# Attention values as the fixed operand in column strips, with outputs that come out turned and scaled

## The chip, the cores and the metric

One Trainium2 chip, one core. The metric is the device time of one launch in microseconds, as the median of several runs; a profile of one execution stands beside it.

## The reference

A transformer block over 4096 tokens of 256 channels, in float32. Its rows are normalised; then attention and a mixture of experts both read the normalised rows, and both are added to the input:

```python
xn = _layernorm(x, axis=-1)
x = x + attention(xn, ...) + experts(xn, ...)
```

The attention is local, with 8 heads of 32 channels. Tokens form blocks of 12, and a block's queries see their own block and the one before it (24 keys):

```python
q, k, v = xn @ Wq.T, xn @ Wk.T, xn @ Wv.T          # 8 heads of 32; q and k scaled
logits = einsum('bnchd,bnkhd->bhnck', q, k_ctx) + rel_shift(einsum('bnchd,phd->bhncp', q, rel_k))
attn = softmax(tanh(logits / 50) * 50, axis=-1)
out = einsum('bhnck,bnkhd->bnchd', attn, v_ctx) @ Wpost.T
```

The experts: each token goes to the best 2 of 8 experts (256 to 704 to 256 channels, silu gate), weighted by its routing probabilities.

## The kernel before

The program writes one instruction stream for each engine by hand; semaphores (`s_...`) order them.

*Attention part.* The tokens are cut into 38 groups (`NG`) of 9 blocks: 108 queries (`GQ`) and 120 keys (`GK`), with the blocks in an order in which even and odd ones lie apart (`ORDER`). A loop over `s` from 0 to 42 is a software pipeline, and each engine runs it in its own order: stage `s` transposes the rows of group `s+1`, makes queries, keys, value rows and position biases of group `s`, scores of group `s-3`, values of group `s-4`, and the projection and output of group `s-5`. Router logits of 4 tiles are made in each of the stages 4 to 11 (`S_L`). VectorE makes the routing in steps from stage 12 on (`S_R`); from stage 26 on (`S_OH`) its steps are eight batches of one-hot tables, which TensorE multiplies in stages 27 to 34 (`tables`). GpSimd splits one piece of expert weights in each of the stages from 8 on.

TensorE's order in a stage: `tables`, `scores(s-3)`, a logits tile, `values(s-4)`, `rows_v(s)`, `project(s-5)`, `turn_out(s-4)`, `turn_biases(s-2)`, `turn(s+1)`, `queries(s)`, `keys(s)`, `biases(s)`. Scores of one head take 32 rows of TensorE's array (`r = slice(DH * i, DH * (i + 1))`), so heads `i` = 0 to 3 lie in four row strips.

*The values.* ScalarE leaves `ex`, the exponentials, with 120 keys on the partitions and 108 queries per head in the columns. GpSimd multiplies five heads (`HM`) by the mask of block pairs, VectorE the other three, the late ones. `v1` holds 32 value columns a head and a column of ones. In `values` each head's `ex` is the fixed operand and `v1` moves 33 columns, so that PSUM bank 6 gets queries on the partitions, and in column 33 each head's denominator. VectorE takes the reciprocal of the 8 denominators and multiplies (`o_sb`, `s_o`). In `turn_out` TensorE transposes the result back, and in the same step brings the queries from the block order to the token order (`perm_out`). VectorE copies it as two parts, `oT_hi` rounded and `oT_lo` the rest, and `project` multiplies them with the two parts of the weights in three reduced-precision passes for each half of the channels. `res` adds the input rows.

```python
for h in (*range(HM, H), *range(HM)):
    if h == 0:
        pe.wait_ge(s_mk, g + 1)
    head = HC * (h % KD) + h // KD
    ins = mm(psum[0:GQ, 6, head * HV:(head + 1) * HV], ex[0:GK, g % 2, h, :], v1[0:GK, g % 5, head, :],
             True, True)
```

VectorE's order in a stage: the routing step, the reciprocal and product of group `s-4`, the late heads' mask of group `s-3`, the residual sum of group `s-5`, the two parts of `oT`, the copy of turned biases, the rest of the turned rows (`rest_v`), the copy of the keys (`kT`), which the next stage's scores wait for, and the copy of the position biases.

*Expert part.* After the loop TensorE runs the experts block by block, 128 slots at a time.

Of the kernel before, what the change touches and what calls it, by code (L numbers as in the profile page):

```python
# [6 lines left out]
ALU = mybir.AluOpType  # L7
# [6 lines left out]
P = 128  # L14
# [24 lines left out]
HV = DH + 1  # L39
# [45 lines left out]
C_OUT = C_IN + GK  # L85
C_FIRST = C_OUT + GK

# [3 lines left out]
def constants():  # L91
# [16 lines left out]
    c[np.arange(GK), C_OUT + np.roll(row, -PAST)] = 1.0  # L108
# [9 lines left out]
def program(nc, x, pos_t, wq, wk, wv, wpost, wrel, dim_scale, norm_w, router_t, w_raw, alpha, const_d,  # L118
            xn_d, bd_d, w_split, out):
    with ExitStack() as ctx:  # L120
# [19 lines left out]
        vp_w = sb("vp_w", [P, 2, 2, KD, D], F32R)  # L140
        WV, WP = range(2)
# [20 lines left out]
        turns = sb("turns", [P, P + 2 * GK], F32R)  # L162
# [3 lines left out]
        perm_out = turns[0:GK, P + GK:P + 2 * GK]  # L166
# [6 lines left out]
        turns_raw = sb("turns_raw", [P, P + (2 + len(NEAR)) * GK], at=raw_at + 2 * KD * D * 4)  # L173
        near_in = turns_raw[:, P + 2 * GK:P + (2 + len(NEAR)) * GK].rearrange("p (i n) -> p i n", n=GK)
        vp_raw = sb("vp_raw", [P, 2, KD, D], at=raw_at)
# [9 lines left out]
        def tile8(i):  # L185
# [5 lines left out]
                     shb=2 * H * CTX, rep=2 * H * DH, relT=2 * KD * GQ, v1=5 * H * HV, ex=2 * H * GQ, xw=NXW * D, o=D, res=2 * D)  # L191
# [10 lines left out]
        o_m = at_m["o"].rearrange("p (h n) -> p h n", h=H)  # L202
# [5 lines left out]
        v1 = at["v1"].rearrange("p (b h n) -> p b h n", b=5, h=H)  # L208
# [31 lines left out]
        rden = sb("rden", [P, H])  # L240
# [22 lines left out]
        s_oth = sem("s_oth")  # L263
# [55 lines left out]
        s_o = sem("s_o")  # L319
        s_ot = sem("s_ot")  # L320
# [150 lines left out]
        def _(sp):  # L471
# [6 lines left out]
            sp.dma_start(vp_raw[:, WV, :, :], wv.rearrange("(k p) e -> p k e", p=P)).then_inc(s_wv, 16)  # L478
# [5 lines left out]
            sp.wait_ge(s_ini, 6)  # L484
# [6 lines left out]
            sp.dma_start(vp_raw[:, WP, :, :], wpost.rearrange("(k p) e -> p k e", p=P)).then_inc(s_wp, 16)  # L491
# [81 lines left out]
        def _(pool):  # L573
# [45 lines left out]
            rest_vp(WV)  # L619
            pool.dma_start(x_all[:, PARTS[2][0]:PARTS[2][1], :], tile_rows(x, 2)).then_inc(s_x[2], 16)  # L620
            for s in range(NG + 3):
# [27 lines left out]
                if s == 3:  # L649
                    rest_vp(WP)  # L650
# [24 lines left out]
        def _(act):  # L675
# [25 lines left out]
            def load_raw(n):  # L701
                if n < NSPL:
                    e, cols = piece(n)
                    if n == 0:
                        act.wait_ge(s_vpl, 2)
                        act.wait_ge(s_turns, 1)
                        act.wait_ge(s_t, NWIN)
# [35 lines left out]
            round_vp(WV, s_wv)  # L743
# [40 lines left out]
            for s in range(NG + NSTEP):  # L784
# [53 lines left out]
                if s == 2:  # L838
                    round_vp(WP, s_wp)
# [37 lines left out]
        def _(dve):  # L877
# [56 lines left out]
            dve.tensor_copy(turns[:, :], turns_raw[:, 0:P + 2 * GK]).then_inc(s_turns, 1)  # L934
# [205 lines left out]
            for s in range(NG + NSTEP):  # L1140
# [476 lines left out]
```

## Time and profile before

| what | us |
|---|---|
| runs | 823.52, 826.76, 829.49 |
| median | 826.76 |
| profiled execution, device time | 825.49 |
| its span, first to last instruction | 823.7 |
| TensorE busy | 778.6 |
| VectorE busy | 458.5 |
| ScalarE busy | 344.2 |
| GpSimd busy | 408.7 |

The span is cut by time: the attention loop ends near 350 us, the experts fill the rest. Busy time of TensorE counts matmuls that overlap once; the profile shows a full-precision matmul as two records, and a reduced-precision one as one.

### The profile page before, as it was taken

The numbers are of one execution on the slowest core, as the hardware profiler recorded it, in microseconds if no ns is written. First come the engines' busy times: TensorE is split into PE (matmuls) and PEld (weight loads), VectorE is DVE, ScalarE is ACT, GpSimd is POOL, SyncE is SP. The second block draws the span as 40 slices with busy tenths as digits, with TensorE's granted clock in tenths as the row PEclk, the third lists the DMA queues.
The fourth block names the chain that finished last, engine by engine and source line by source line (L and its number), as shares of the span: only waits on it lengthen the run. The fifth ranks groups of instructions, "written<-read, shape, count | busy, mean of one in ns | idle before, by whom it ended". The sixth has DMA issues, their size and how long they took to land.

```text
span 823.7 us, 20450 instructions
## 1 busy us (share of the span) xinstructions
PE 778.6 (95%) x6909; PEld 750.2 (91%) x6909; DVE 458.5 (56%) x1057; ACT 344.2 (42%) x620; POOL 408.7 (50%) x307
## 2 busy tenths in 40 slices
PE   6599999999899999899999999999999999999993
PEld 6599999999799998899999999999999999999993
DVE  5464358888788855454444444444444444444441
ACT  4456666666545466333333333333333333333330
POOL 2777867777846667513333333333333333333322
PEclk9799999999999999799999999999999999999997
DMA  8645788899954463112264363363363462222211
GB/s 254 186 129 163 242 267 281 300 300 310 307 197 137 127 137 89 36 31 40 40 175 120 83 177 69 69 182 80 71 174 87 119 175 39 35 39 41 37 26 24
DMA packets 65798, 111.07 MB, mean 135 GB/s; under 512 B 15640, under 2 KB 47812, under 8 KB 65700
## 3 DMA queue, kind: packets, MB, share of 16 engines
q0 software_dynamic: 19536, 44.22, 22.4%
q1 hardware_dynamic: 34644, 45.03, 18.6%
q10 hardware_dynamic: 11520, 20.47, 7.5%
q8 instruction: 67, 1.10, 0.6%
q14 instruction: 31, 0.25, 0.1%
HBM read 66.97 MB, written 42.75 MB: 133 GB/s over the span
## 4 chain that ended last, share of the span: by engine, by line
PE 85%; DMA 3%; DVE 3%; issue 2%; POOL 2%; ACT 1%; ACTq 1%; SPq 1%; POOLq 0%; DVEq 0%
PE psum L1251 77%; PE psum L1359 4%; PE psum L1322 1%; POOL xn_all L611 1%; DMA arena<-in_x 1%; DMA out<-spare,sca_i 1%; DVE arena L1196 1%; PE psum L1435 1%; ACTq L752 1%; DMA q_scale<-in_dim_scale 1%; PE psum L1295 1%; PE psum L1444 1%; PE psum L1270 1%; DVE xT L1111 1%; ACT xT L755 0%
## 5 line engine op out<-in xcount | busy, mean ns | idle before, releaser
L1251 PE MATMUL psum<-w_ring,xT 128*128 x1608 | 278.4, 329 | 4.3 <-DVE xT L1111 1.5
L1251 PEld LDWEIGHTS psum<-w_ring,xT 128*128 128x128 f32 x1608 | 258.0, 189 | 17.4 <-issue 15.1
L657 POOL DMA_INDIRECT out<-spare,sca_i x67 | 106.3, 1586 | 273.7 <-DVE spare L1235 248.9
L1100 DVE SCALAR_TENSOR_TENSOR spare<-psum,xg,spare 128x704 f32<-128x704 f32 x67 | 63.7, 951 | 161.4 <-PE psum L1251 161.2
L1251 PE MATMUL psum<-w_ring,hT 128*128 x1139 | 151.6, 286 | 2.1 <-DVE spare L1235 1.4
L1251 PEld LDWEIGHTS psum<-w_ring,hT 128*128 128x128 f32 x1139 | 140.2, 190 | 2.4 <-issue 2.4
L857 ACT ACTIVATE spare<-psum,xg 128x704 f32<-128x704 f32 x67 | 56.8, 847 | 159.8 <-PE psum L1251 159.8
L755 ACT ACTIVATE xT<-psum,nwp 128x128 fp32r<-128x128 f32 x134 | 41.9, 364 | 159.0 <-PE psum L1322 142.6
L635 POOL TENSOR_TENSOR arena<-arena,const 120x540 f32<-120x540 f32 x38 | 59.9, 1576 | 71.7 <-ACT arena L801 71.6
L1251 PE MATMUL psum<-arena 32*120 32x108 f32 (+1 forms) x1216 | 87.7, 265 | 0.0
L594 POOL DMA_INDIRECT xg<-xn_d,gat_i x67 | 70.4, 1051 | 32.3 <-issue 19.1
L1251 PEld LDWEIGHTS psum<-arena 32*120 32x120 f32 (+1 forms) x1216 | 82.7, 181 | 2.8 <-issue 0.2
L585 POOL TENSOR_TENSOR w_ring<-raw,w_ring 128x1088 fp32r<-128x1088 f32 x32 | 84.7, 2646 | 0.0
L1251 PE MATMUL psum<-arena,att_w 128*128 128x120 f32 (+1 forms) x608 | 82.4, 288 | 0.0
L1251 PEld LDWEIGHTS psum<-arena,att_w 128*128 128x128 f32 x608 | 75.2, 200 | 0.0
L1111 DVE SCALAR_TENSOR_TENSOR xT<-psum,nwp,xT 128x128 fp32r<-128x128 f32 x134 | 40.9, 347 | 57.8 <-ACT xT L755 57.8
L1223 DVE TENSOR_TENSOR hT<-psum,hT 128x768 fp32r<-128x768 f32 x67 | 64.2, 958 | 7.3 <-ACT hT L865 1.5
L797 ACT ACTIVATE psum<-psum 120x864 f32<-120x864 f32 x38 | 33.3, 876 | 55.5 <-PE psum L1251 55.0
L865 ACT ACTIVATE hT<-psum 128x768 fp32r<-128x768 f32 x67 | 54.4, 811 | 4.9 <-PE psum L1359 4.9
L1359 PEld LDWEIGHTS psum<-turns,hb_m 128*128 128x128 f32 x402 | 41.4, 140 | 1.7 <-issue 0.3
L1359 PE MATMUL psum<-turns,hb_m 128*128 128x128 f32 x402 | 42.0, 241 | 0.1
L577 POOL TENSOR_TENSOR arena<-arena 120x256 f32<-120x256 f32 x38 | 31.6, 833 | 17.6 <-DMA arena<-in_x 17.5
(171 smaller groups left out, 1000.1 us busy)
## 6 DMA issues: line engine op xcount, KB each, us to landing
w_split<-w_ring POOLq DMA_DIRECT2D x20, 1088.0 KB, 6.7
w_ring<-w_split SPq DMA_DIRECT2D x40, 544.0 KB, 3.8
raw<-in_w_raw ACTq DMA_DIRECT2D x32, 544.0 KB, 5.9
arena<-xn_d SPq DMA_DIRECT2D x34, 120.0 KB
arena<-in_x SPq DMA_DIRECT2D x37, 108.0 KB
out<-arena SPq DMA_DIRECT2D x37, 108.0 KB
bd_d<-arena SPq DMA_DIRECT2D x38, 84.4 KB
xn_d<-xn_all POOLq DMA_DIRECT2D x3, 1024.0 KB, 7.5
```

The costliest lines, as they stand in the source:

```text
L585: pool.tensor_tensor(lo, raw[:, n % NST, :], hi.bitcast(F32), ALU.subtract).then_inc(s_spl, 1)
L594: pool.indirect_dma_start(out=xg[:, b % NXG, :], out_offset=None, in_=xn_d, in_offset=bass.IndirectOffsetOnAxis(ap=gat_i[:, b:b + 1], axis=0),
L635: pool.tensor_tensor(ex[0:GK, g % 2, 0:HM, :], ex[0:GK, g % 2, 0:HM, :], mask.rearrange("p (a n) -> p a n", a=1).to_broadcast([GK, HM, GQ] ...
L657: pool.indirect_dma_start(out=out, out_offset=bass.IndirectOffsetOnAxis(ap=sca_i[:, b:b + 1], axis=0), in_=y[:, b % 2, :], in_offset=None, ...
L755: ins = act.activation(xT[:, b % 2, HI, k, :], psum[:, x_bank(b), k * P:(k + 1) * P], ACT.Copy, scale=nwp[:, k:k + 1])
L857: act.activation(sg[:, b % 2, :].rearrange("p (a n) -> p a n", a=2), psum[:, 0:2, 0:HALF], ACT.Silu, scale=xg[:, b % NXG, D:D + 1]).then_i ...
L865: act.activation(hT[:, b % 2, HI, :, :].rearrange("p (a k) n -> p a (k n)", a=2), psum[:, 4:6, 0:3 * P], ACT.Copy).then_inc(s_hta, 1)
L1100: dve.scalar_tensor_tensor(out=hb[:, b % 2, 0:HID].rearrange("p (a n) -> p a n", a=2), in0=psum[:, 2:4, 0:HALF], scalar=scale, in1=sg[:, b ...
L1111: ins = dve.scalar_tensor_tensor(out=xT[:, b % 2, LO, k, :], in0=psum[:, x_bank(b), k * P:(k + 1) * P], scalar=nwp[:, k:k + 1], in1=xT[:, ...
L1223: dve.tensor_tensor(hT[:, b % 2, LO, :, :].rearrange("p (a k) n -> p a (k n)", a=2), psum[:, 4:6, 0:3 * P], hT[:, b % 2, HI, :, :].bitcast ...
L1251: return pe.matmul(out_ap, lhs, rhs, start=first, stop=last)
L1359: ins = pe.transpose(moved(psum[:, 4 + c // 3, (c % 3) * P:(c % 3 + 1) * P]), hb_m[:, b % 2, c * P:(c + 1) * P], ident_m)
```

## The change

The two operands of the values' products change places. Each head's 32 value columns are the fixed operand, and its 108 columns of `ex` move; the result lands on 32 partitions of bank 6, channels on the partitions, so the four heads of one half of the channels lie in four column strips of the array. A second product for each head, with 32 columns of ones as the fixed operand, puts the head's denominators beside it, one copy on each of the 32 partitions. So 8 products of a group become 16, and their order is: the three late heads' values, their denominators, then the other five by halves. VectorE takes the reciprocal of all 216 columns of denominators and multiplies in two steps (odd and even blocks), which write the queries in token order. The output transposes (`turn_out`, `perm_out`), `o_sb`, and the two parts of `oT` go; `oT` is double-buffered, in plain float32. `project` becomes one full-precision product for each half of the channels, with the projection weights as loaded; ScalarE's and GpSimd's steps that split those weights in stages 2 and 3 go. The fills of `v1`'s ones and of `o_sb` become one of `oT`.

```diff
-        vp_w = sb("vp_w", [P, 2, 2, KD, D], F32R)
-        WV, WP = range(2)
+        wv_w = sb("wv_w", [P, 2, KD, D], F32R)
+        wp_w = sb("wp_w", [P, KD, D])
...
-        v1 = at["v1"].rearrange("p (b h n) -> p b h n", b=5, h=H)
+        v = at["v"].rearrange("p (b h n) -> p b h n", b=5, h=H)
...
-        o_sb = at["o"].rearrange("p (h n) -> p h n", h=H)
+        rden = at["rden"][:, 0:KD * GQ]
         res = at["res"].rearrange("p (b d) -> p b d", b=2)
         xv = sb("xv", [P, 2, KD, GK], F32R)
-        oT_hi = sb("oT_hi", [P, KD, GK], F32R)
-        oT_lo = sb("oT_lo", [P, KD, GK], F32R)
+
+        oT = sb("oT", [P, 2, KD, GK])
...
-            pool.memset(v1[:, :, :, DH:HV], 1.0).then_inc(s_ini, 1)
-            pool.memset(o_sb[:, :, :], 0.0).then_inc(s_ini, 1)
+            pool.memset(oT[:, :, :, :], 0.0).then_inc(s_ini, 1)
...
-                if s == 3:
-                    rest_vp(WP)
...
-                if s == 2:
-                    round_vp(WP, s_wp)
...
-                    pv = psum[0:GQ, 6, 0:H * HV].rearrange("p (h n) -> p h n", h=H)
-                    dve.reciprocal(rden[0:GQ, :], pv[:, :, DH:HV].rearrange("p h n -> p (h n)")).then_inc(s_rc, 1)
+                    if g == 0:
+                        dve.wait_ge(s_ini, 5)
+                    if g >= 2:
+                        dve.wait_ge(s_po, g - 1)
+                    dve.reciprocal(rden, psum[:, 6, KD * GQ:2 * KD * GQ]).then_inc(s_rc, 1)
                     dve.wait_ge(s_rc, g + 1)
-                    if g:
-                        dve.wait_ge(s_ot, g)
-                    dve.tensor_tensor(o_sb[0:GQ, :, :], pv[:, :, 0:DH],
-                                      rden[0:GQ, :].rearrange("p (h n) -> p h n", n=1).to_broadcast([GQ, H, DH]),
-                                      ALU.mult).then_inc(s_o, 1)
+
+                    place = oT[:, g % 2, :, :].rearrange("p k (m a c) -> p k m a c", a=2, c=CHUNK)
+                    for first, n, m, a in ((0, NODD, 1, 0), (NODD, NEVEN, 0, 1)):
+                        cols = slice(first * CHUNK, (first + n) * CHUNK)
+                        num, den = (t.rearrange("p (k n) -> p k n", k=KD)[:, :, cols].rearrange("p k (m c) -> p k m c", c=CHUNK)
+                                    for t in (psum[:, 6, 0:KD * GQ], rden))
+                        ins = dve.tensor_tensor(place[:, :, m:m + n, a, :], num, den, ALU.mult)
+                    ins.then_inc(s_ote, 1)
...
-                    dve.wait_ge(s_ot, g + 1)
-                    if g:
-                        dve.wait_ge(s_po, g)
-                    o_ps = psum[:, 6, 0:KD * GK].rearrange("p (k n) -> p k n", k=KD)
-                    dve.tensor_copy(oT_hi[:, :, :], o_ps).then_inc(s_oth, 1)
-                    dve.wait_ge(s_oth, g + 1)
-                    dve.tensor_tensor(oT_lo[:, :, :], o_ps, oT_hi[:, :, :].bitcast(F32), ALU.subtract).then_inc(s_ote, 1)
...
-                for h in (*range(HM, H), *range(HM)):
-                    if h == 0:
-                        pe.wait_ge(s_mk, g + 1)
-                    head = HC * (h % KD) + h // KD
-                    ins = mm(psum[0:GQ, 6, head * HV:(head + 1) * HV], ex[0:GK, g % 2, h, :], v1[0:GK, g % 5, head, :],
-                             True, True)
+
+                def products(heads, of):
+                    for h in heads:
+                        i, k = h // KD, h % KD
+                        at = (KD * of + k) * GQ
+                        lhs = ones[0:GK, 0:DH] if of else v[0:GK, g % 5, HC * k + i, :]
+                        ins = mm(psum[DH * i:DH * (i + 1), 6, at:at + GQ], lhs, ex[0:GK, g % 2, h, :], True, True)
+                    return ins
+
+                late = range(HM, H)
+                products(late, 0)
+                products(late, 1)
+                pe.wait_ge(s_mk, g + 1)
+                for first in range(KD):
+                    products(range(first, HM, KD), 0)
+                    ins = products(range(first, HM, KD), 1)
...
-                    pe.wait_ge(s_vpl, 2)
+                    pe.wait_ge(s_wp, 16)
                 if g:
                     pe.wait_ge(s_r2, g)
                 for k in range(KD):
-                    for po, pw in PASSES:
-                        ins = mm(psum[0:GK, 7, 0:D], (oT_hi, oT_lo)[po][:, k, :], vp_w[:, pw, WP, k, :],
-                                 k == 0 and (po, pw) == PASSES[0], k == KD - 1 and (po, pw) == PASSES[-1])
+                    ins = mm(psum[0:GK, 7, 0:D], oT[:, g % 2, k, :], wp_w[:, k, :], k == 0, k == KD - 1)
...
-            def turn_out(g):
-
-                pe.wait_ge(s_o, g + 1)
-                for k in range(KD):
-                    ins = pe.matmul(moved(psum[:, 6, k * GK:(k + 1) * GK]),
-                                    o_m[0:GK, HC * k:HC * (k + 1), :].rearrange("p h n -> p (h n)"), perm_out,
-                                    start=True, stop=True, is_transpose=True)
-                ins.then_inc(s_ot, 1)
...
-                    turn_out(s - 4)
```

## Rows read from the trace of the kernel before

**Rows 1.** The profile's page: the chain that ended last, shares of the span by engine.
```profile
PE 85%; DMA 3%; DVE 3%; issue 2%; POOL 2%; ACT 1%; ACTq 1%; SPq 1%; POOLq 0%; DVEq 0%
```

**Rows 2.** Stretches: length, busy us (instructions) by engine, granted clock, DMA share, GB/s.
```profile
43.20:117.60 74.40, 73.67 (x868) 71.61 (x869) 35.57 (x106) 47.10 (x95) 57.57 (x48) 1.00 0.62 196
117.60:218.90 101.30, 98.44 (x1217) 94.68 (x1216) 81.75 (x212) 67.67 (x115) 76.36 (x54) 1.00 0.90 299
218.90:232.20 13.30, 8.89 (x89) 8.61 (x90) 11.50 (x15) 4.70 (x9) 7.61 (x7) 0.87 0.80 277
232.20:302.70 70.50, 70.31 (x816) 68.18 (x814) 57.08 (x116) 37.67 (x64) 43.28 (x24) 1.00 0.50 139
```

**Rows 3.** Timeline of stage 24, TensorE: start us, us, line, tiles, shape, [idle before].
```profile
204.65 0.68 PE L1251 MATMUL psum<-arena,const 32*120 32x108 f32 x16 [0.22 <-DVE arena L1196]
...
207.22 0.96 PE L1251 MATMUL psum<-vp_w,xv 128*120 128x256 f32 x6
208.02 0.40 PE L1251 MATMUL psum<-vp_w,oT_hi 128*120 128x256 f32 x2
...
208.73 0.28 PE L1444 MATMUL psum<-turns,arena_m 120*128 120x120 f32 x2
208.85 0.33 PE L1435 MATMUL psum<-turns,arena_m 108*128 108x108 f32 x2
...
209.19 2.02 PE L1251 MATMUL psum<-arena,att_w 128*128 128x108 f32 x16
...
211.80 0.63 PE L1251 MATMUL psum<-arena,const 32*120 32x108 f32 x13 [0.22 <-DVE arena L1196]
```

**Rows 4.** Timeline of stage 26 and the start of stage 27, TensorE and VectorE.
```profile
226.81 0.20 DVE L1153 RECIPROCAL rden<-psum 108x8 f32<-108x8 f32 x1
...
227.52 0.36 PE L1444 MATMUL psum<-turns,arena_m 120*128 120x120 f32 x2 [4.38 <-DVE arena L1157]
...
228.06 3.64 PE L1251 MATMUL psum<-arena,att_w 128*128 128x108 f32 x16
...
233.97 0.68 PE L1251 MATMUL psum<-arena,const 32*120 32x108 f32 x16
```

**Rows 5.** Timeline of a logits stage, TensorE.
```profile
80.26 0.68 PE L1251 MATMUL psum<-arena,const 32*120 32x108 f32 x16
80.76 0.60 PE L1251 MATMUL psum<-arena 32*120 32x108 f32 x16
81.29 0.61 PE L1251 MATMUL psum<-rt_w,spare 128*128 128x8 f32 x4
```

**Rows 6.** Timeline of the expert counts, TensorE, full precision, and their group with the mean ns.
```profile
153.70 1.05 PE L1251 MATMUL psum<-spare,const 128*128 128x256 f32 x4
...
L1251 PE MATMUL psum<-spare,const 128*128 128x256 f32 x4 | 1.1, 386 | 0.0
```

**Rows 7.** Groups by line and shape: busy us, mean ns of one.
```profile
L1005 DVE RECIPROCAL small<-small 128x32 f32<-128x32 f32 x1 | 0.4, 353 | 0.0
...
L912 DVE RECIPROCAL small<-small 128x4 f32<-128x4 f32 x2 | 0.3, 169 | 0.0
...
L912 DVE RECIPROCAL small<-small 128x16 f32<-128x16 f32 x1 | 0.2, 239 | 0.0
...
L912 DVE RECIPROCAL small<-small 128x8 f32<-128x8 f32 x1 | 0.2, 203 | 0.3 <-ACT small L683 0.3
```

**Rows 8.** Timeline of stage 24, VectorE.
```profile
207.43 0.21 DVE L1153 RECIPROCAL rden<-psum 108x8 f32<-108x8 f32 x1 [2.28 <-PE psum L1251]
...
208.01 0.48 DVE L1163 TENSOR_TENSOR arena<-arena,const 120x324 f32<-120x324 f32 x1
208.93 0.42 DVE L1175 TENSOR_TENSOR arena<-psum,arena 120x256 f32<-120x256 f32 x1 [0.44 <-PE psum L1251]
...
211.24 0.41 DVE L1196 TENSOR_SCALAR arena<-psum 128x240 f32<-128x240 f32 x1 [0.52 <-PE psum L1251]
```

**Rows 9.** Groups by line and shape in the 14 plain stages.
```profile
L1163 DVE TENSOR_TENSOR arena<-arena,const 120x324 f32<-120x324 f32 x14 | 15.2, 1086 | 0.0
```

More of the change, by code:

```diff
@@ L38 @@
 ORDER = list(range(-1, GB, 2)) + list(range(0, GB, 2))
-HV = DH + 1
 E, HID = 8, 704
@@ L84 @@
 C_IN = C_ID + P
-C_OUT = C_IN + GK
-C_FIRST = C_OUT + GK
+C_FIRST = C_IN + GK
 NEAR = ((0, 0), (1, 0), (1, 1), (2, 1), (2, 2))
@@ L107, in constants @@
     c[row, C_IN + np.arange(GK)] = 1.0
-    c[np.arange(GK), C_OUT + np.roll(row, -PAST)] = 1.0
     for i, (g, t) in enumerate(NEAR):
@@ L159, in program @@
         keys_of = const[:, C_REP:C_REP + GK]
-        turns = sb("turns", [P, P + 2 * GK], F32R)
+        turns = sb("turns", [P, P + GK], F32R)
         xg_m = sb("xg_m", [P, NXG, DX], F32R, at=xg_at)
@@ L172, in program @@
         raw = sb("raw", [P, NST, PC])
-        turns_raw = sb("turns_raw", [P, P + (2 + len(NEAR)) * GK], at=raw_at + 2 * KD * D * 4)
-        near_in = turns_raw[:, P + 2 * GK:P + (2 + len(NEAR)) * GK].rearrange("p (i n) -> p i n", n=GK)
-        vp_raw = sb("vp_raw", [P, 2, KD, D], at=raw_at)
+        turns_raw = sb("turns_raw", [P, P + (1 + len(NEAR)) * GK], at=raw_at + 2 * KD * D * 4)
+        near_in = turns_raw[:, P + GK:P + (1 + len(NEAR)) * GK].rearrange("p (i n) -> p i n", n=GK)
+        wv_raw = sb("wv_raw", [P, KD, D], at=raw_at)
         xn_all = sb("xn_all", [P, TT, D], at=ring_at)
@@ L477, in _ @@
             sp.dma_start(turns_raw[:, :], const_d[:, C_ID:C_FIRST + len(NEAR) * GK]).then_inc(s_tr, 16)
-            sp.dma_start(vp_raw[:, WV, :, :], wv.rearrange("(k p) e -> p k e", p=P)).then_inc(s_wv, 16)
+            sp.dma_start(wv_raw[:, :, :], wv.rearrange("(k p) e -> p k e", p=P)).then_inc(s_wv, 16)
             load_part(1)
@@ L483, in _ @@
             sp.dma_start(wrel_s, wrel.rearrange("(k p) e -> p k e", p=P)).then_inc(s_rb, 16)
-            sp.wait_ge(s_ini, 6)
+            sp.wait_ge(s_ini, 5)
             for g in range(NWIN):
@@ L617, in store_xn @@
                 pool.dma_start(tile_rows(xn_d, i), xn_all[:, first:last, :]).then_inc(s_xnst[i], 16)
-            rest_vp(WV)
+            rest_wv()
             pool.dma_start(x_all[:, PARTS[2][0]:PARTS[2][1], :], tile_rows(x, 2)).then_inc(s_x[2], 16)
@@ L704, in load_raw @@
                     if n == 0:
-                        act.wait_ge(s_vpl, 2)
+                        act.wait_ge(s_vpl, 1)
                         act.wait_ge(s_turns, 1)
@@ L732, in round_piece, with round_wv @@
                 act.activation(w_ring[:, split_slot(e), HI, cols], raw[:, n % NST, :], ACT.Copy).then_inc(s_hi, 1)
-            def round_vp(i, loaded):
-                act.wait_ge(loaded, 16)
-                act.activation(vp_w[:, HI, i, :, :], vp_raw[:, i, :, :], ACT.Copy).then_inc(s_vph, 1)
+            def round_wv():
+                act.wait_ge(s_wv, 16)
+                act.activation(wv_w[:, HI, :, :], wv_raw[:, :, :], ACT.Copy).then_inc(s_vph, 1)
             def load_part(i):
@@ L742, in _ @@
             deviation(0)
-            round_vp(WV, s_wv)
+            round_wv()
             act.wait_ge(s_nb, 1)
@@ L770, in repeat @@
                 if g == 0:
-                    act.wait_ge(s_ini, 6)
+                    act.wait_ge(s_ini, 5)
                 if g >= 2:
@@ L813, in _ @@
                     if s == 0:
-                        act.wait_ge(s_ini, 6)
+                        act.wait_ge(s_ini, 5)
                     if s >= 5:
                         act.wait_ge(s_pv, s - 4)
-                    act.activation(v1[0:GK, s % 5, :, 0:DH], psum[0:GK, 5, 0:D].rearrange("p (h n) -> p h n", h=H),
+                    act.activation(v[0:GK, s % 5, :, :], psum[0:GK, 5, 0:D].rearrange("p (h n) -> p h n", h=H),
                                    ACT.Copy).then_inc(s_ve, 1)
@@ L933, in _ @@
             dve.wait_ge(s_tr, 16)
-            dve.tensor_copy(turns[:, :], turns_raw[:, 0:P + 2 * GK]).then_inc(s_turns, 1)
+            dve.tensor_copy(turns[:, :], turns_raw[:, 0:P + GK]).then_inc(s_turns, 1)
             tile_stats(*CHUNKS[1])
```

21 lines of the change are left out of this document (6 added, 15 removed).

## The prediction

> **What bounds the kernel now.** I read the chain of work that ended last first: 85% of it is TensorE [rows 1]. Next come four stretches of the attention part [rows 2], cut where a stage ends; how many stages each holds follows from the loop's constants. Stages 4 to 11 also carry router logits (8 in 74.4 us, 9.30 each), 12 to 25 are plain (14 in 101.3 us, 7.24 on average), stage 26 takes 13.3, 27 to 34 carry the routing tables' products (8 in 70.5 us, 8.81). Three plain stages and a drain with the last four groups' values follow. The expert part behind them, 60% of the span, is not edited. So x us saved in a stage count up to 34 times, if TensorE's queue is what each stage waits for. In the logits and table stages it is: TensorE is busy for 73.7 of 74.4 and 70.3 of 70.5 us [rows 2]. In a plain one, of 7.15 us (204.65 to 211.80), it waits 0.22 us, for VectorE's key copy [rows 3]. In stage 26 it stands 4.38 us at the output transposes, because VectorE works off one-hot tables first and divides afterwards; then it needs 3.64 us for the queries and keys that take 2.02 in a plain stage, and the mean granted clock of the stretch is 0.87, so TensorE, after that idle time, ran partly at the lower of its two levels (1.2 GHz) [rows 2 to 4].
>
> **The change on TensorE.** Every full-precision product is two records: 8 heads show as 16. *Values* take 1.54 us now: from scores to value rows it is 204.65 to 207.22, 2.57 us [rows 3], and the 32 score records take 1.03 of it (80.26 to 81.29 [rows 5]). That is 96 ns a record although only 33 columns move, so the 108-column fixed operand sets it. Afterwards there are 16 products, 32 records, each moving 108 columns under 32 fixed ones. Four records of 256 moving columns take 1.05 us in all and 0.386 each on average, so they follow each other after (1.05 - 0.386)/3 = 0.22 us [rows 6], and 108 columns cost 0.22 x 108/256 = 93 ns. One after another that is 32 x 93 = 3.0 us. No column strip is in this trace. The nearest rows are the row strips of the scores: 16 records in 0.50 us, 31 ns each [rows 5], a third of what the values' records take one after another, so strips do work side by side. Each column strip gets exactly 8 records; full overlap is 8 x 93 = 0.74 us, and I allow one record, 0.1, for changing between strips and full width. The three late heads use strips 2, 3 and 3, twice, before strips 0 and 1 get anything; if the queue keeps that order strictly, with one record waiting per strip, I count 14 slots of 93 ns, 1.4 us with the allowance. Bounds 0.85 to 1.4 with overlap, 3.0 without; I take 1.1, the middle of the former, as the row strips are nearest: -0.44.
> *Projection*: six records take 0.71 us now (208.02 to 208.73); four of 256 columns at 0.22 take 0.88: +0.17. *Output transposes*: 0.12 us (208.73 to 208.85) go [rows 3]. Sum on TensorE: -0.39 a stage.
>
> **The change on VectorE.** A reciprocal of 8 columns, a product, a cast and a difference go, and a reciprocal over 216 columns and two products of 96 and 120 columns come. Reciprocals of 16 and 32 columns take 239 and 353 ns, 7.1 ns a column, so 216 cost 0.353 + 184 x 0.0071 = 1.66 us; the bounds are 1.56 (slope from 4 to 32 columns) and 1.9 (slope from 4 to 8) [rows 7]. The Trainium skill's page "VectorE: DVE Perf Modes" (walkthrough, fixed hardware budget) says that the reciprocal repeats its divide step 8 times. At that page's 0.96 GHz, 216 columns are an estimated 1.80 us, and the total would come some 2 us later; the rows give less per column, and I go by them. The two products cost about 0.18 and 0.20, in line with the key copy's 0.41 for 240 columns less what neighbours overlap.
>
> Where that lies: from the reciprocal to the key copy it is 207.43 to 211.24 now, 3.81 us, of which VectorE idles 0.44 + 0.52 [rows 8]: the cover is under 1 us. Of the 2.85 us of work the four steps that go are about 1.35 (each takes 0.21 to 0.42); 1.66 + 0.03 + 0.38 = 2.07 come. With the late heads' mask M written apart (0.48 in this stage, 0.40 up to the next start), the rest is 1.1. The chain of a plain stage becomes: scores 1.03, values V, to the reciprocal 0.21 (207.22 to 207.43), 2.07, M, 1.1, key copy 0.41, to the next scores 0.15 (211.24 + 0.41 to 211.80): 4.9 + V + M [rows 3, 8]. The mask averages 1.09 us over the 14 stages [rows 9], so M is 1.0. With V = 1.1 that is 7.0, plus about 0.2 where a routing step is longer than the time before the values end: 7.2. TensorE alone would allow 7.15 - 0.39 = 6.76.
>
> **Sum by kind of stage**, for V = 1.1. Logits stages, TensorE-bound: 8 x -0.39 = -3.1. Plain ones: nothing, since VectorE, at 7.2, now sets them. The last three plain ones, without routing: 3 x -0.37 = -1.1. Table stages: VectorE is busy 57.08 us in 8, 7.1 each [rows 2]; with 0.7 more it still fits under 8.42, so 8 x -0.38 = -3.0. Stage 26: with the transposes gone nothing on TensorE waits there for the division, so queries, keys and the first table products run under VectorE's tables, which end at 226.81 [rows 4]. What is late next is the key copy: 226.81 + 2.07 + 0.9 + 1.1 + 0.41 = 231.3, scores at 231.4, against 233.97 now [rows 4]. That is 2.6 less; I take -2.5 (bounds -3 to -1, as TensorE then idles in another place and its clock may fall there).
> The drain: the values shorten by 0.44, the way from reciprocal to projection swaps 1.35 us of VectorE and the transposes for 2.07, the projection is longer: nothing, within 2 us either way. At the start ScalarE's rounding of the projection weights and GpSimd's subtraction behind it go; both queues then hold loads and layer norms, and TensorE waits for other loads there: nothing to -1. The projection's new wait for its weights stands on a load issued some stages earlier, and the fills stay about as large: nothing. Total -9.7.
>
> **Rivals.** (1) *VectorE becomes the bound and the kernel gets slower.* The mask moves behind the long reciprocal, into GpSimd's weight splitting; if it then takes 1.3 us throughout and the reciprocal 1.9, the plain chain is 4.9 + 0.25 + 1.1 + 1.22 + 0.4 = 7.9, +0.65 x 14 = +9, the table stages are +0.2 x 8, the logits stages keep their -3, stage 26 its -2: +5, 832. It decides once V + M passes 2.1 us, which is where the forecast puts it. For it speaks that VectorE is busy 81.75 of 101.3 us in the plain stages already [rows 2]; against it that the mask can take 0.48 [rows 8]. The Trainium skill's "TensorEngine Tiling (Array Packing)", section on performance, warns of this: packing speeds the products, not what empties PSUM.
> (2) *Strips start in program order and hold each other up*: V = 1.4. Logits and table stages -0.1 each, plain ones +0.25 each, stage 26 -2: about 0, 827. The Trainium skill's "TensorE: Matmul & The Clock Gate", part 3, says that matmuls keep strict order in start and end. The score records follow each other after 31 ns, but they change strip regularly and no row names it, so no run here shows that yet.
> (3) *Two strips at a time*: V = 16 x 0.093 + 0.2 = 1.7; logits and tables +0.2 x 16 = +3, plain ones +0.6 x 14 = +8, stage 26 -2, the last three +1: 837.
> (4) *No overlap; the change doesn't do what it says*: V = 3.05, +1.55 on TensorE: 16 x 1.55 = 25 in logits and table stages, the plain chain 4.9 + 3.05 + 1.2 = 9.1, +1.9 x 14 = 27, the last three +5, the drain 4 x 1.5 = 6, stage 26 -1: +62, 889. For it: nothing here shows full precision in column strips, where each strip must stream all 120 rows. Against it: the row strips.
>
> **How the numbers follow.** The profiled execution took 825.49 us, 1.8 beyond its span and 1.3 below the median of the three runs; I put the difference on the median: 826.8 - 9.7 = 817.1. Forecast 0.48, with V from 0.85 (reciprocal at its lower bound, plain stages -0.5: -20, 806) to 1.25 (823). Rival (1) 0.17, (2) 0.10, (3) 0.07, (4) 0.18. The range 806 to 838 leaves out rival (4) and the tails of (1) and (3), about 0.21. One per cent, about what a measurement here can tell, is 8.3 us: below 818.5 lies some 0.32, all from the forecast; within 1% the rest of it, (2) and most of (1), 0.38; above 835 (3), (4) and the tail of (1), 0.30.
>
> **What would show it.** From the value records to the value rows 1.1 us, or 3.0; four projection records 0.22 apart; one reciprocal near 1.66 us; logits stages near 8.9 us; plain ones near 7.2, their wait for the key copy longer than 0.22; no 4.38 us gap in stage 26. If the values take over 1.4 us, or plain stages pass 7.4, the forecast is wrong.

## The result and the profile after

The changed kernel takes 832.2 us (median of 16 runs) against 826.4 for the kernel before: ratio 1.0086, 95% interval 1.0069 to 1.0102. The forecast was 817.1; it became slower. Medians here are over all runs of a kernel, ratios leave out the runs more than 1.5% above its fastest. The profiled execution took 834.16 us, its span 832.4, 8.7 above the span of before (823.7). The page of the changed kernel, its chain and two of its groups, against [rows 1] and [rows 9]:

```profile
PE 68%; DVE 14%; issue 7%; DMA 6%; ACT 2%; SPq 1%; ACTq 1%; POOL 0%; DVEq 0%; POOLq 0%
...
L1142 DVE RECIPROCAL arena<-psum 128x216 f32<-128x216 f32 x38 | 57.2, 1506 | 46.5 <-PE psum L1234 44.3
...
L1155 DVE TENSOR_TENSOR arena<-arena,const 120x324 f32<-120x324 f32 x38 | 61.4, 1615 | 0.1
```

TensorE's share of the chain fell from 85 to 68%, VectorE's rose from 3 to 14. The new reciprocal takes 1.51 us. The second group is VectorE's mask of the late heads, which the change doesn't touch: 1.62 us on average over all stages. In the 14 plain stages alone, for which [rows 9] has 1086 ns, it is 2067:

```profile
L1155 DVE TENSOR_TENSOR arena<-arena,const 120x324 f32<-120x324 f32 x14 | 28.9, 2067 | 0.0
```

The stretches of the changed kernel, cut at key copies, with the columns of [rows 2]; the fifth is stage 10 alone, the last the first 36.8 us behind the last key copy:

```profile
40.40:118.10 77.70, 75.30 (x965) 69.17 (x964) 44.96 (x99) 47.08 (x95) 55.35 (x47) 0.96 0.58 187
118.10:234.70 116.60, 99.86 (x1388) 90.50 (x1388) 97.60 (x198) 65.72 (x115) 72.23 (x55) 0.96 0.76 259
234.70:246.30 11.60, 9.15 (x118) 8.19 (x116) 11.50 (x13) 5.07 (x9) 8.00 (x7) 1.00 0.90 319
246.30:315.40 69.10, 66.57 (x894) 61.79 (x895) 66.80 (x108) 36.15 (x64) 39.08 (x24) 1.00 0.52 144
97.00:108.90 11.90, 11.37 (x115) 10.36 (x115) 4.17 (x11) 4.93 (x11) 5.72 (x5) 0.71 0.83 306
336.20:373.00 36.80, 31.84 (x351) 27.96 (x350) 19.61 (x38) 14.16 (x22) 15.71 (x11) 0.91 0.15 42
```

The same cuts by the key copies' times in each trace (us; the last three kernels are experiments, below):

| stretch | before | after | wait (e8) | PSUM mask (e11) | e11 with strips (e12) |
|---|---|---|---|---|---|
| start, to stage 4 | 42.7 | 40.4 | 41.4 | 42.0 | 42.7 |
| 8 logits stages | 74.4 | 77.7 | 73.2 | 73.7 | 72.8 |
| 14 plain stages | 101.3 | 116.6 | 104.4 | 98.2 | 95.9 |
| stage 26 | 13.3 | 11.6 | 9.7 | 8.9 | 8.8 |
| 8 table stages | 70.5 | 69.1 | 76.0 | 66.7 | 63.6 |
| last three | 21.2 | 20.8 | 21.0 | 20.8 | 20.7 |
| drain and experts | 500.3 | 496.2 | 493.0 | 491.6 | 493.1 |

All the loss lies in the plain stages, +15.3 us, and in the logits stages 9 and 10, which the table's second line holds. In the plain stretch TensorE is now busy for 99.86 of 116.6 us, where it was 98.44 of 101.3. One such stage, all engines, cut to what matters:

```profile
136.10 0.68 PE L1234 MATMUL psum<-arena,const 32*120 32x108 f32 x16 [1.93 <-DVE arena L1179]
...
138.40 0.97 PE L1234 MATMUL psum<-wv_w,xv 128*120 128x256 f32 x6
...
138.57 1.51 DVE L1142 RECIPROCAL arena<-psum 128x216 f32<-128x216 f32 x1 [0.43 <-PE psum L1234]
...
139.13 1.34 POOL L625 TENSOR_TENSOR arena<-arena,const 120x540 f32<-120x540 f32 x1 [3.05 <-ACT arena L789]
139.21 1.02 PE L1234 MATMUL psum<-wp_w,oT 128*120 128x256 f32 x4
139.89 0.47 PE L1426 MATMUL psum<-turns,arena_m 108*128 108x108 f32 x2
...
140.12 0.45 DVE L1150 TENSOR_TENSOR oT<-psum,arena 128x96 f32<-128x96 f32 x2
...
140.37 2.02 PE L1234 MATMUL psum<-arena,att_w 128*128 128x108 f32 x16
...
140.43 2.49 POOL L576 TENSOR_TENSOR w_ring<-raw,w_ring 128x1088 fp32r<-128x1088 f32 x1
140.48 2.79 DVE L1155 TENSOR_TENSOR arena<-arena,const 120x324 f32<-120x324 f32 x1
...
143.20 0.41 DVE L1167 TENSOR_TENSOR arena<-psum,arena 120x256 f32<-120x256 f32 x1
...
144.14 0.39 DVE L1179 TENSOR_SCALAR arena<-psum 128x240 f32<-128x240 f32 x1
...
144.68 0.68 PE L1234 MATMUL psum<-arena,const 32*120 32x108 f32 x16 [1.93 <-DVE arena L1179]
```

The mask, 0.48 us where nothing stands beside it [rows 8], is issued 0.05 us behind GpSimd's subtraction of a weight piece and ends 0.35 us behind that one's end (142.92, 143.27). In stage 12 it is issued 0.52 us behind (123.79 against 123.27), takes 2.33 us and again ends 0.35 us behind the subtraction. VectorE then comes to the key copy, for which TensorE waits 1.93 us instead of 0.22 [rows 3]. The stage lasts 8.58 us. Two stages on, the same two stand the other way round, and in the kernel before the mask stands ahead of the subtraction, behind GpSimd's own mask. The changed kernel, then the one before:

```profile
157.58 0.48 DVE L1155 TENSOR_TENSOR arena<-arena,const 120x324 f32<-120x324 f32 x1
157.59 2.84 POOL L576 TENSOR_TENSOR w_ring<-raw,w_ring 128x1088 fp32r<-128x1088 f32 x1
```
```profile
142.84 1.34 POOL L635 TENSOR_TENSOR arena<-arena,const 120x540 f32<-120x540 f32 x1 [1.32 <-ACT arena L801]
143.23 1.30 DVE L1163 TENSOR_TENSOR arena<-arena,const 120x324 f32<-120x324 f32 x1
144.15 2.75 POOL L585 TENSOR_TENSOR w_ring<-raw,w_ring 128x1088 fp32r<-128x1088 f32 x1
```

In these records whichever of the two engines comes first works at its full pace, and the other's record is longer by what it stood: the mask by up to 2.3 us, the subtraction by 0.35. That the changed stage with the 0.48 us mask lasts 6.86 us, 0.28 less than 7.14 before, shows what the change would give in a plain stage without this.

### The profile page after: what moved, and what is told of

Its sections match the earlier page's. It is cut to its first block, busy times and chain, and to the rows that moved or that the text cites. A ratio compares the mean times of both kernels' runs of the same rounds, so it can differ in the third digit from the quotient of the medians.

```text
span 832.4 us, 21273 instructions
## 1 busy us (share of the span) xinstructions
PE 772.6 (93%) x7365; PEld 729.3 (88%) x7365; DVE 495.2 (59%) x1019; ACT 341.1 (41%) x619; POOL 397.6 (48%) x305
## 4 chain that ended last, share of the span: by engine, by line
PE 68%; DVE 14%; issue 7%; DMA 6%; ACT 2%; SPq 1%; ACTq 1%; POOL 0%; DVEq 0%; POOLq 0%
PE psum L1234 62%; DVE arena L1142 4%; PE psum L1342 3%; DMA w_ring<-w_split 3%; DVE arena L1155 2%; DVE spare L1064 1%; PE psum L1305 1%; DVE arena L1179 1%; DVE arena L1167 1%; DMA out<-spare,sca_i 1%; DVE xv L1107 1%; DVE arena L1116 1%; DMA wv_raw<-in_wv 1%; DMA arena<-xn_d 1%; DMA arena<-in_x 1%
## 5 line engine op out<-in xcount | busy, mean ns | idle before, releaser
L1234 PEld LDWEIGHTS psum<-w_ring,xT 128*128 128x128 f32 x1608 | 257.3, 189 | 15.7 <-issue 15.3
L843 ACT ACTIVATE spare<-psum,xg 128x704 f32<-128x704 f32 x67 | 56.9, 849 | 158.1 <-PE psum L1234 158.1
L625 POOL TENSOR_TENSOR arena<-arena,const 120x540 f32<-120x540 f32 x38 | 53.4, 1404 | 99.3 <-ACT arena L789 99.3
L1234 PE MATMUL psum<-arena,const 32*120 32x108 f32 (+1 forms) x1216 | 72.5, 278 | 22.2 <-DVE arena L1179 22.2
L1142 DVE RECIPROCAL arena<-psum 128x216 f32<-128x216 f32 x38 | 57.2, 1506 | 46.5 <-PE psum L1234 44.3
L576 POOL TENSOR_TENSOR w_ring<-raw,w_ring 128x1088 fp32r<-128x1088 f32 x32 | 83.0, 2595 | 0.0
L1234 PEld LDWEIGHTS psum<-arena,const 32*120 32x120 f32 (+1 forms) x1216 | 54.6, 148 | 28.1 <-issue 27.3
L1234 PE MATMUL psum<-arena 32*120 32x108 f32 (+1 forms) x1216 | 69.5, 273 | 0.8 <-DVE arena L1155 0.8
L1155 DVE TENSOR_TENSOR arena<-arena,const 120x324 f32<-120x324 f32 x38 | 61.4, 1615 | 0.1
```

What stands on the lines that cost most here:

```text
L576: pool.tensor_tensor(lo, raw[:, n % NST, :], hi.bitcast(F32), ALU.subtract).then_inc(s_spl, 1)
L625: pool.tensor_tensor(ex[0:GK, g % 2, 0:HM, :], ex[0:GK, g % 2, 0:HM, :], mask.rearrange("p (a n) -> p a n", a=1).to_broadcast([GK, HM, GQ] ...
L843: act.activation(sg[:, b % 2, :].rearrange("p (a n) -> p a n", a=2), psum[:, 0:2, 0:HALF], ACT.Silu, scale=xg[:, b % NXG, D:D + 1]).then_i ...
L1142: dve.reciprocal(rden, psum[:, 6, KD * GQ:2 * KD * GQ]).then_inc(s_rc, 1)
L1155: dve.tensor_tensor(ex[0:GK, g % 2, HM:H, :], ex[0:GK, g % 2, HM:H, :], mask.rearrange("p (a n) -> p a n", a=1).to_broadcast([GK, H - HM, ...
L1234: return pe.matmul(out_ap, lhs, rhs, start=first, stop=last)
```

## The experiments

The first four change GpSimd's order and the order of the strips.

e1, GpSimd subtracts first in each stage and masks afterwards:
```diff
+                for n in pieces(s):
+                    split(n)
                 if 0 <= s - 3 < NG:
                     g = s - 3
                     pool.wait_ge(s_ex, g + 1)
...
-                    split(n)
+                    store_split(n)
```


> The changed kernel with one order turned: from stage 8 on GpSimd subtracts its piece of expert weights before the heads' mask, and issues the store and the sum of input rows after it. Theory P (a VectorE mask cannot run while a GpSimd tensor instruction runs; the 1.5 us reciprocal moved it behind the start of GpSimd's subtraction): the mask falls from 1.7 to 2.8 us to about 0.5, plain stages from 8.6 to about 6.9, total near 812 us. Theory L (VectorE just has more work than fits): nothing of VectorE's own work changes, plain stages stay at 8.6, total 830 to 834.

849.6 us, ratio to before 1.0288 (1.0259 to 1.0318). A miss. GpSimd's queue and the row that explains it:
```profile
127.10 2.52 POOL L576 TENSOR_TENSOR w_ring<-raw,w_ring 128x1088 fp32r<-128x1088 f32 x1 [7.85 <-ACT w_ring L728]
129.58 1.51 POOL L631 TENSOR_TENSOR arena<-arena,const 120x540 f32<-120x540 f32 x1
```
The subtraction waits for ScalarE's rounding of the piece, 7.85 us here and 56.9 in all, and GpSimd's mask, on which the values depend, is queued behind it. The order itself costs, so this says nothing on the collision.

e2, the products of the values in strip order, after both masks:
```diff
-                late = range(HM, H)
-                products(late, 0)
-                products(late, 1)
                 pe.wait_ge(s_mk, g + 1)
-                for first in range(KD):
-                    products(range(first, HM, KD), 0)
-                    ins = products(range(first, HM, KD), 1)
+                for k in range(KD):
+                    products(range(k, H, KD), 0)
+                    ins = products(range(k, H, KD), 1)
```


> The changed kernel with the 16 value products in strip order 0, 1, 2, 3 throughout, and both masks waited for ahead of them. Theory H (strips start in program order and hold each other up): from scores to value rows 2.0 us in place of 2.3 to 2.5, every TensorE-bound stage 0.3 us shorter. With theory P the mask then is issued some 0.3 us earlier, ahead of GpSimd's subtraction (it came 0.05 us behind its start), so it takes 0.5 to 1.3 us and plain stages fall below 7 us: total 805 to 815. With theory L only the 0.3 us a stage show: about 822. If strips do not hold each other up: 832.

829.2 us, ratio 1.0032 (1.0000 to 1.0064), above theory P's 805 to 815. The profiled execution, 819.9 us, is the fastest of the ten. In it most logits stages come to 8.77 us from 9.15. Of the 14 plain ones seven take 6.5 us, with masks of 0.5 to 0.8, and three 8.6 to 8.9, with masks of 2.4 to 2.7; the other four lie between 7.4 and 14.4. So the order of the strips is worth 0.38 us in a logits stage, and the collision stays in some of the plain ones.

e3, both edits:

> Both edits of the two runs before: GpSimd's subtraction ahead of the mask, and strips in turn. P and H together: values 1.0 us, mask 0.5 us, plain stages 6.5 to 6.6, logits stages 8.8, total 800 to 808. L: about 822.

848.3 us, ratio 1.0289 (1.0209 to 1.0369): as e1, and a miss too.

e4, the order of e1 in the kernel before:

> The kernel before, with GpSimd's order turned in the same way. P: its plain stages are bound by TensorE with a VectorE mask of 0.5 to 1.3 us, so only the mask gets shorter, not the stage: 7.1 us, total within 3 us of the kernel before; so the order alone is no gain without the change. If the order is worth as much here as in the changed kernel (15 us or more), the loss was not the reciprocal's.

866.9 us, ratio 1.0516 (1.0460 to 1.0571), where a time within 3 us of the kernel before was expected: a miss. GpSimd waits for ScalarE's rounding in 30 stages there, 84.3 us in all. In this order, bad for both, the changed kernel is 17 us faster than the one before.

The next four leave GpSimd's order as it was. e8 has it wait for VectorE's mask before it subtracts:
```diff
+                if 0 <= s - 3 < NG:
+                    pool.wait_ge(s_mkd, s - 2)
                 for n in pieces(s):
                     split(n)
```


> The changed kernel, with one wait added: GpSimd begins its subtraction of a weight piece in a stage only when VectorE's mask of that stage is done. Nothing else is moved. Theory P (the loss is VectorE's mask, which the longer reciprocal puts just behind the start of the 2.49 us subtraction and which is then held to that one's end): VectorE's masks take about 0.5 us in all plain stages, and these stages, 8.6 to 9.2 us from key copy to key copy in the changed kernel, come to 6.9 to 7.1; the two stages 9 and 10 stay above (9.3 to 9.8 in the kernel before). 12 stages by about 1.8 us and some 4 us of the other two, less about 4 us given back to the experts' stage: 808 to 815 us, faster than both kernels. Theory Q (the weights' splitting is itself what sets the stages, and the mask only waits in its place): masks 0.5 us, stages still 8.2 to 8.6, 828 to 834 us.

822.5 us, ratio 0.9948 (0.9920 to 0.9975). The masks are 0.49 us in all plain and table stages but one (1.20, in stage 14), the plain stages 6.9 to 7.7 but for three of 8.4 to 8.7: theory P on the cause, but only half its gain. The table stages show where the rest went, VectorE and GpSimd of one of them:
```profile
287.37 2.49 POOL L576 TENSOR_TENSOR w_ring<-raw,w_ring 128x1088 fp32r<-128x1088 f32 x1 [3.77 <-DVE arena L1157]
288.73 1.73 DVE L1065 TENSOR_TENSOR xg<-const,small 128x568 f32<-128x568 f32 x1
...
291.73 1.60 POOL L625 TENSOR_TENSOR arena<-arena,const 120x540 f32<-120x540 f32 x1 [0.68 <-ACT arena L791]
292.05 1.88 DVE L1067 TENSOR_TENSOR xg<-xg,small 128x568 f32<-128x568 f32 x1
293.96 0.75 DVE L1068 TENSOR_TENSOR xg<-xg,const 128x568 f32<-128x568 f32 x1
```
The subtraction, put off, now holds up the one-hot tables: an instruction of 0.73 us in the changed kernel takes 1.73 beside it. Another of 0.74 takes 1.88 beside GpSimd's mask. The eight stages take 76.0 us instead of 69.1. In the three long plain stages it is routing steps: in two of them the first, 0.4 us elsewhere, takes 1.41 beside the subtraction.

e9, the same with the strips in order:

> The same wait, and the products of the values in strip order (both masks waited for first, then heads 0 and 4, 1 and 5, and so on over the four strips) instead of GpSimd's five heads ahead of VectorE's three. If the hold-up of strips in program order is worth what the logits stages showed when only the order was changed (9.15 to 8.77 us, 0.38 a stage), the 8 logits stages gain 0.38 each and the plain ones 0.2 to 0.38 over the kernel with the wait alone: 5 to 10 us below it, about 800 to 810 us. If the wait for both masks costs as much as the order gives: equal to it within 2 us. Theory Q: 826 to 832 us.

818.1 us, ratio 0.9877 (0.9828 to 0.9926): 4 us below e8 by the medians and 5.9 by the ratios, at the low end of the 5 to 10 expected, and above the 800 to 810 that were to come of it. Its table stages are 9.7 to 10.3 us, as long as e8's.

e10, the wait in the kernel before:

> The kernel before, with the same wait of GpSimd's subtraction for VectorE's mask: the control. Theory P: its mask stands ahead of the subtraction anyhow in most plain stages (1.09 us on average in 14 of them against 0.48 where nothing is beside it), so that the wait can give at most 0.6 us in each of 14 stages: 818 to 826 us; what the changed kernel gains by the wait (some 20 us) is several times that, and the change, both with the wait, is then 6 to 15 us faster than no change. Theory Q: the wait costs the kernel before as much as it costs the changed one, 826 to 834 us.

822.8 us, ratio 0.9947 (0.9924 to 0.9970). Most plain stages keep their 7.12 to 7.16 us and the masks their 1.3, which GpSimd's mask sets; stage 26 is 9.6 us, 3.8 less. So with the wait in both the change is worth nothing (822.5 against 822.8), not the 6 to 15 us expected. Between the two profiled executions e8's plain stages are 3.0 us longer than e10's (104.4 against 101.4) and its table stages 5.6 longer; drain and experts are 6.5 shorter, start and logits stages 1.7 and 1.8.

e6, a reciprocal of 8 of the 216 columns:
```diff
-                    dve.reciprocal(rden, psum[:, 6, KD * GQ:2 * KD * GQ]).then_inc(s_rc, 1)
+                    dve.reciprocal(rden[:, 0:8], psum[:, 6, KD * GQ:KD * GQ + 8]).then_inc(s_rc, 1)
```


> The changed kernel, with the reciprocal of 8 of the 216 columns alone (0.2 us in place of 1.51); the other denominators are taken as one, so most of the division is left out. The products that follow stand. Theory P: VectorE reaches its mask 1.3 us earlier, ahead of the subtraction's start, behind GpSimd's own mask (1.34 us) at most; the mask takes 0.5 to 1.4 us and the plain stages come to 6.9 to 7.3: 808 to 818 us. If the reciprocal's length isn't what puts the mask behind the subtraction (the products or GpSimd's order are): masks of 1.7 to 2.8 us stay, and the time is 826 to 832 us.

808.4 us, ratio 0.9779 (0.9736 to 0.9823), and plain stages mostly of 6.87 us.
```profile
136.73 1.34 POOL L625 TENSOR_TENSOR arena<-arena,const 120x540 f32<-120x540 f32 x1 [1.08 <-ACT arena L789]
136.80 1.62 DVE L1156 TENSOR_TENSOR arena<-arena,const 120x324 f32<-120x324 f32 x1
138.03 2.75 POOL L576 TENSOR_TENSOR w_ring<-raw,w_ring 128x1088 fp32r<-128x1088 f32 x1
```
The mask, issued earlier, stands only behind GpSimd's mask and is through before the subtraction, as in the kernel before.

The last four ask what is held. In e8 VectorE's copies and additions out of PSUM ran beside the subtraction at 0.35 to 0.42 us; only instructions with all operands in SBUF were long. e11 has the mask read its 0s and 1s from a corner of bank 6 (9 columns, each used for the 12 of a chunk); order and waits stay:
```diff
+        mask_p = psum[0:GK, 6, 496:496 + GB]
...
+            dve.wait_ge(s_const, 16)
+            link(dve.tensor_copy(mask_p, mask[:, 0:GQ:CHUNK]))
...
-                    dve.tensor_tensor(ex[0:GK, g % 2, HM:H, :], ex[0:GK, g % 2, HM:H, :],
-                                      mask.rearrange("p (a n) -> p a n", a=1).to_broadcast([GK, H - HM, GQ]),
-                                      ALU.mult).then_inc(s_mkd, 1)
+                    mine = ex[0:GK, g % 2, HM:H, :].rearrange("p h (j c) -> p h j c", c=CHUNK)
+                    dve.tensor_tensor(mine, mine, mask_p.rearrange("p (h j c) -> p h j c", h=1, c=1).to_broadcast(
+                        [GK, H - HM, GB, CHUNK]), ALU.mult).then_inc(s_mkd, 1)
```


> The changed kernel, with VectorE's mask reading its mask (9 columns, each used for the 12 of a chunk) from a corner of PSUM instead of SBUF; no order and no wait is changed, so the mask still starts just behind GpSimd's subtraction. Theory P2 (only VectorE instructions whose operands are all in SBUF wait for GpSimd's instruction to end; the copies and additions that read PSUM ran at 0.35 to 0.42 us beside the same subtraction in the last kernels): the mask takes 0.5 to 0.6 us in every stage, the plain stages of 8.6 to 9.2 us come to 6.9, the table stages of 8.9 to 7.2 to 8.0, and the time to 793 to 808 us. Rival Q2 (a running GpSimd instruction holds any VectorE instruction that writes SBUF, or any with two operands, wherever they are read): masks of 1.7 to 2.8 us stay, 828 to 834 us.

e14, the control, reads the same 9 columns from SBUF (`mask_s = const[0:GK, C_MASK:C_MASK + GQ:CHUNK]`):

> The control to the mask in PSUM: the same instruction with the 9 columns, each used for 12, read from SBUF. P2: as the changed kernel, masks of 1.7 to 2.8 us in the same stages, 829 to 834 us. If the form of the operand (9 columns used over and over) and not its place is what frees the mask: as the run with the mask in PSUM.

e11: 806.9 us, ratio 0.9779 (0.9741 to 0.9817). e14: 834.1 us, 1.0104 (1.0072 to 1.0136). The group of the mask and one stage in e11, then the group in e14:
```profile
L1159 DVE TENSOR_TENSOR arena<-arena,psum 120x324 f32<-120x324 f32 x38 | 18.3, 481 | 0.7 <-ACT arena L790 0.7
...
141.99 2.51 POOL L577 TENSOR_TENSOR w_ring<-raw,w_ring 128x1088 fp32r<-128x1088 f32 x1
142.06 0.48 DVE L1159 TENSOR_TENSOR arena<-arena,psum 120x324 f32<-120x324 f32 x1
```
```profile
L1157 DVE TENSOR_TENSOR arena<-arena,const 120x324 f32<-120x324 f32 x38 | 67.0, 1763 | 0.0
```
One operand's place makes 481 ns of 1763. The mask stands 0.07 us behind the subtraction's start, as in the changed kernel, and neither is lengthened. The stretches of e11, as above:
```profile
115.70:213.90 98.20, 95.55 (x1388) 86.50 (x1388) 82.12 (x198) 65.76 (x115) 71.30 (x54) 1.00 0.91 306
213.90:222.80 8.90, 8.68 (x117) 8.10 (x116) 8.80 (x13) 5.15 (x9) 6.97 (x6) 1.00 0.89 307
222.80:289.50 66.70, 66.36 (x897) 61.66 (x897) 59.29 (x109) 36.14 (x64) 40.74 (x26) 1.00 0.59 160
310.30:347.10 36.80, 31.87 (x371) 28.27 (x370) 20.68 (x43) 15.31 (x24) 14.66 (x11) 1.00 0.15 43
```
The Trainium skill states this rule on the page "SBUF — State Buffer", section "SBUF: two separate sides": VectorE and GpSimd share one pair of SBUF ports, and whichever starts first, a GpSimd instruction that reads SBUF or a VectorE one with two SBUF inputs, has it for the whole instruction while the other is fully blocked. The records agree: 2.79 us beside 2.49 with two SBUF inputs, 0.48 with one of the two in PSUM. Which of the two starts first the records don't tell that finely: in e15, below, a mask whose record starts 0.08 us behind isn't held. The table stages of e11 come to 8.5 us in six of eight, not to the 7.2 to 8.0 expected. The same edit in the kernel before wasn't tried.

e12, e11 with the strips in order:

> The same, and the products of the values in strip order behind both masks. Under P2 GpSimd's mask of five heads (1.34 us) is now the later of the two, so waiting for both costs little, and each stage gains the 0.38 us that the logits stages gained by the order alone: 8 logits stages and some 20 others, 8 to 11 us below the run with the mask in PSUM, 783 to 799 us. Under Q2 as the strips alone, 819 to 830 us.

Ratio 0.9797 (0.9759 to 0.9835), median 811.5 us over runs from 799.5 to 823.9: not told apart from e11, and the 8 to 11 us below it are not there. In its profiled execution (799.45 us, the fastest of its six) the logits stages are mostly 8.8 and the plain ones 6.5 to 7.4. One of these, TensorE:
```profile
142.98 0.68 PE L1237 MATMUL psum<-arena,const 32*120 32x108 f32 x16 [0.38 <-DVE arena L1182]
...
144.22 0.37 PE L1237 MATMUL psum<-arena,const 120*32 120x108 f32 x8
144.41 0.37 PE L1237 MATMUL psum<-arena 120*32 120x108 f32 x8
144.59 0.37 PE L1237 MATMUL psum<-arena,const 120*32 120x108 f32 x8
144.89 0.97 PE L1237 MATMUL psum<-wv_w,xv 128*120 128x256 f32 x6
```

e15 adds the suspected cost to the kernel before:
```diff
                     dve.reciprocal(rden[0:GQ, :], pv[:, :, DH:HV].rearrange("p h n -> p (h n)")).then_inc(s_rc, 1)
+                    dve.reciprocal(unread[0:GQ, :], psum[0:GQ, 6, 0:184])
```


> The kernel before, with one unread reciprocal of 184 columns of PSUM put behind its reciprocal of 8 (about 1.3 us, so that VectorE's division lasts as long as the changed kernel's, while TensorE does what it did). Theory P2 (the loss is the place to which the longer division moves the mask): the masks of the plain stages, 1.3 us where GpSimd's own mask holds them, fall into the subtraction and take 1.7 to 2.8 us; the plain stages go from 7.14 to 8.6 to 9.2 us, and 14 of them with stage 26 make 20 to 30 us: 846 to 857 us. Rival (only the reciprocal's own length is paid, 1.3 us less the 0.96 us for which VectorE stands idle in a plain stage): plain stages of 7.5 to 7.7 us, 14 by 0.4 to 0.6 and 1.3 in stage 26: 832 to 837 us.

874.8 us, ratio 1.0539 (1.0473 to 1.0606), beyond both. A plain stage, and two stretches (logits stages 10 and 11 with the plain stage behind them, and four of the plain ones):
```profile
174.04 2.94 POOL L586 TENSOR_TENSOR w_ring<-raw,w_ring 128x1088 fp32r<-128x1088 f32 x1
174.12 0.48 DVE L1165 TENSOR_TENSOR arena<-arena,const 120x324 f32<-120x324 f32 x1
```
```profile
107.50:153.70 46.20, 45.68 (x308) 44.78 (x309) 15.26 (x37) 16.45 (x33) 16.63 (x13) 0.52 0.48 170
161.40:192.90 31.50, 29.57 (x351) 27.47 (x351) 24.80 (x63) 18.82 (x33) 22.73 (x17) 1.00 0.85 276
```
The masks stay at 0.48 us in most plain stages, though they start 0.01 to 0.19 us behind the subtraction, and the plain stages mostly take 7.7, the rival's figure. Of the 48.0 us by which the span grows, 19.7 are three stages that TensorE, after 1.34 us of idle time, runs almost wholly at its lower level (0.52 granted, 46.2 us for what takes 26.5 before). TensorE also waits at the output transposes, which the changed kernel doesn't have, for the later products: 14.0 us in all. So the length of the division does not by itself make the mask wait for the subtraction.

## Why the prediction was wrong

**The step that failed** is M, the mask in the plain chain 4.9 + V + M: "The mask averages 1.09 us over the 14 stages, so M is 1.0." Its records were 0.48 alone and 1.30 behind GpSimd's mask, so 1.09 was the mean of a work and of a wait for another engine, and a wait isn't carried over when the instruction moves. Moved to where the subtraction starts, it averages 2.07 us over the same 14 stages (28.9 us in all), and these stages, forecast to stay as long as they were, take 15.3 us more. (The chain's constant was also added up short: its terms make 4.97, not 4.9.) Rival (1) named the place and the direction, and 832 us, but by a mask of 1.3 throughout and a plain stage of 7.9; it is 2.07, and 8.6 to 9.2 in 11 of the 14 (+15.3 us for its +9, and +3.3 for its -3 in the logits stages). That its total came out near was luck: drain and experts, start and table stages, 7.8 us shorter together, were put at +2. What the Trainium skill's page "SBUF — State Buffer", section "SBUF: two separate sides", says of the shared ports belonged in the prediction beside [rows 8, 9].

**V** was 1.1 of 0.85 to 1.4. In the changed kernel the scores take 1.03 us of the 2.30 from 136.10 to 138.40, so V is 1.27; in strip order it is 144.89 - 142.98 - 1.03 = 0.88. Both counts of the prediction come near (1.4 if strips hold each other up in program order, 0.84 if not) and the kernel is near the former: the mechanism of rival (2) was also true. Most logits stages gave 0.15 us and not 0.39; in e2, by the order alone, it is 0.53. In stages 9 and 10 even that went: a mask of 4.62 us, under an addition, GpSimd's mask and a subtraction, and after the idle time a stage of 11.9 us at a granted clock of 0.71, +4.2 us for the two against before.

**What held.** The strips work side by side, and rivals (3) and (4) fall. The reciprocal is 1.51 us (forecast 1.66, lower bound 1.56). A plain stage without the collision is 6.86 us, 0.28 less, where VectorE was to hold it at 7.2: there it still stands idle 0.56 us at the key copy. From value rows to queries it is 1.97 us (138.40 to 140.37), as before [rows 3], where the projection and the transposes were to add 0.05: the projection takes 0.68 us (139.21 to 139.89) and not 0.88, and the transposes' 0.12 are lost again between the turned biases and the queries (0.48 us for 0.34). Stage 26 gave 1.7 us of 2.5, and 4.4 in e11. The table stages gave 1.4 of 3.0 with masks of 2.19 us, 3.8 in e11.

**What came unforeseen.** The drain was put at 0 within 2, the experts at nothing; together they gave 4.1 us, 8.7 in e11. The experts' first product comes 17.7 us behind the last key copy before, 15.8 in the changed kernel and 14.3 in e11, so about half of it or more lies in the experts, whose code is the same. The granted clock of the 16 us from 330 is 0.68 before; over the first 36.8 us behind the last key copy it is 0.86 before, 0.91 after, 1.00 in e11. Why TensorE keeps its level there is not shown. The start's 2.3 us are no more than what traces of one and the same start differ by: the fourth key copy stands at 40.1 us in e1 and at 42.3 in e2.

With the collision out of the way (e11), the median is 25.3 us below the changed kernel's and 19.5 below that of before: the change with one operand moved is the faster kernel, by 2.2%. How much of this the operand alone would give the kernel before is not known. An estimate for the four stretches of [rows 2] is some 8 us: so long TensorE stands idle in them (0.7, 2.9, 4.4 and 0.2 us).

**Open**: why the mask loses at 0.04 to 0.06 us behind the subtraction's record in the changed kernel and wins at up to 0.19 in e15; within two tenths of a microsecond the records don't tell which of the two has to wait.

## What to carry to other kernels

A duration that varies in the trace holds a wait: split its records by what ran beside them before carrying the mean to a new place. When an edit lengthens work ahead of an instruction with all operands in SBUF, look up which GpSimd instruction will then be running, and allow for a stall of that one's whole remainder. Here moving the GpSimd instruction moved the stall to the next such instruction, and reading one operand from PSUM ended it. Issue products in column strips so that neighbours use different strips: in the logits stages this was worth 0.38 us each, though in the whole e12 isn't told apart from e11.

## What the runs showed of the hardware

The two engines don't share by degrees: at the hand-over less than a tenth of a microsecond between their records in the changed kernel decides between a mask of 0.48 us with a subtraction of 2.84 and one of 2.79 with 2.49. It isn't two-operand instructions alone: a conversion and a scalar step of 128x32 in SBUF, 0.18 us each in the changed kernel's routing, took 1.0 and 1.2 us in e8's, beside GpSimd instructions. And 1.3 us of idle TensorE time stood ahead of stages that cost several: 11.9 us for 9.15 in stage 10 of the changed kernel, 46.2 for 26.5 in e15, both at a lower granted clock (0.71 and 0.52). But the plain stages from 127.0 to 144.1 us, with 1.93 us of idle time each, kept 1.00; what makes the difference is not shown.
